# Expert loops that turn and copy tokens four tiles ahead, and results added to x by accumulating transfers

## The chip, the cores and the metric

The kernel runs on one core of a Trainium2 chip. What counts is the time of one execution on the device, in microseconds (us). The kernel before takes 1687.06 us, the median of three runs (1686.94 to 1687.19).

## What is computed

The reference carries a tensor x of 64 × 64 tokens with 128 features (f32) through eight stages, four attentions in turn with four feed-forward stages. Each stage adds its result to x, and normalizes x for its own input. The change touches three of the feed-forward stages. All three have eight experts with weights 128 × 512 and 512 × 128, and a router that picks for every token the one expert (f0) or the two experts (f1, f3) with the highest score:

```python
x = x + _L0_ffn_ref(_layernorm(x), ...)   # f0: top-1 of 8, gelu, no biases
x = x + _L1_ffn_ref(_layernorm(x), ...)   # f1: top-2 of 8, gelu, biases b1, b2
x = x + _L3_ffn_ref(_layernorm(x), ...)   # f3: top-2 of 8, relu, biases; its sum is the output
# one expert:  y = act(x @ W1[e] + b1[e]) @ W2[e] + b2[e];  out += gate * y
```

The fourth, f2, lets 16 experts choose their tokens. It has code of its own, and the change leaves it alone.

## The kernel before

x stays in SBUF as 32 tiles of 128 tokens. A routing step sorts the tokens by expert into tiles of 128 slots (padded: 39 tiles in f0, 71 in f1 and in f3), and writes the normalized tokens with their gates to DRAM (`d_xn`). `m.src` holds for each slot the row to fetch, `m.dst` the row of `d_y` for its result, `m.expert` the expert of each tile.

`experts(k, m)` (from L929) is a software pipeline over the tiles n. Each engine has a program of its own, and semaphores hold them together:

- GpSimd (POOL in the profile) gathers the tokens of tile n+6 (L964) and then scatters the results of tile n to `d_y` (L968). `xs` and `y` are rings of four tiles each. Its program is written out tile by tile.
- TensorE (PE) does for tile n in this order: the up projection of tile n+2 (L998) out of `xsT`, turning the tokens of tile n+3 (L991), and the down projection of tile n (L1006). Its results alternate between two PSUM banks of each kind: `BT` for turned tokens, `BH` for the hidden layer, `BY` for the output.
- ScalarE (ACT) copies the turned tokens of tile n+3 from PSUM into `xsT` (L1037), which has two buffers, computes the activation of tile n+2 (L1047) and copies the weights of the expert of tile n+4 (L1032).
- VectorE (DVE) keeps the gates of tile n+3 (L1086, L1088), reads the expert's number (L1072) and adds the bias to the hidden layer of tile n+2 (L1077), and for tile n adds the second bias (L1104) and multiplies by the gate (L1108). f0 has no biases, so neither L1077 nor L1104.

PE, ACT and DVE run a loop in hardware (`Fori`, in `groups`) whose body is a group of four tiles; the first and the last group stand written out.

Each result has its place in `d_y`: partition, choice, tile. After `experts` comes `combine(k, m, out)` (L1117) in a block of its own, before which all engines meet. SP loads the results in quarters of eight tiles, 512 KB each, four of them for each choice (L1142). GpSimd adds the second choice to x, and DVE the first (L1133; in f0, with one choice, the two share the quarters). Behind it DVE takes the statistics of each tile (`tile_stats`, L85) for the next normalization. In f3 there are none of these; SP stores x as the output (L1146).

Of the kernel before, what the change touches and what calls it, by code (L numbers as in the profile page):

```python
# [15 lines left out]
P = 128  # L16
# [651 lines left out]
def wait(eng, sem, value):  # L668

    if not isinstance(value, int) or value > 0:  # L670
        eng.wait_ge(sem, value)
# [256 lines left out]

def experts(k, m):  # L929

# [6 lines left out]
    with ExitStack() as st:  # L937
        def sb(name, shape, dt=F32):
            return st.enter_context(nc.sbuf_tensor(f"{tag}_{name}", shape, dt))
        xs = sb("xs", [P, RX, GROW])  # L940
        slot_gate = sb("slot_gate", [P, RX])
        xsT = sb("xsT", [P, 2, P])
        w1e = sb("w1e", [P, RT, FF])
# [7 lines left out]
            "x_turned", "x_copied", "w_copied", "up_done", "biased", "activated", "down_done", "y_ready", "gate_kept", "y_summed")]  # L951
        up_read = activated if m.b1 is None else biased

        def groups(eng, body):

            body(0)
            with eng.Fori(1, I - 1) as i:
                body(i)
            body(I - 1, turn=LAST, end=True)
        with nc.Block() as block:  # L960
            @block.gpsimd
            def _(pool):
                def gather(n, u):
                    nc.gpsimd.indirect_dma_start(xs[:, u % RX, :], None, k.d_xn,  # L964
                                                 bass.IndirectOffsetOnAxis(m.src[:, n:n + 1], 0)).then_inc(gathered[u % RX], 16)

                def scatter(n, u):
                    nc.gpsimd.indirect_dma_start(k.d_y, bass.IndirectOffsetOnAxis(m.dst[:, n:n + 1], 0),  # L968
                                                 y[:, u % RT, :], None).then_inc(scattered[u % RT], 16)
                for n in range(AHEAD):  # L970
                    wait(pool, x_turned, n - RX + 1)
                    wait(pool, gate_kept, n - RX + 1)
                    gather(n, n)
                for n in range(N):
                    if n + AHEAD < N:
                        wait(pool, gate_kept, n + AHEAD - RX + 1)
                        gather(n + AHEAD, n + AHEAD)
                    pool.wait_ge(y_ready, n + 1)
                    scatter(n, n)
                for u in range(RT):  # L980
                    pool.wait_ge(scattered[u], 16 * len(range(u, N, RT)))

            @block.tensor
            def _(pe):
# [8 lines left out]
                def up_proj(n, u):  # L993
                    pe.wait_ge(w_copied, n + 1)
                    pe.wait_ge(x_copied, n + 1)
                    wait(pe, up_read, n - 1)
                    for s in range(HS):
                        last = nc.tensor.matmul(BH[u % 2][:, s * P:(s + 1) * P], w1e[:, u % RT, s * P:(s + 1) * P],  # L998
                                                xsT[:, u % 2, :], start=True, stop=True)
                    last.then_inc(up, 1)  # L1000
# [8 lines left out]

                def body(i, turn=RX, end=False):  # L1010
                    for u in range(turn):
                        n = RX * i + u
                        e = expert_of(n)
                        if not end or u + 2 < turn:
                            up_proj(n + 2, u + 2)
                        if not end or u + 3 < turn:
                            turn_x(n + 3, u + 3, i + (u + 3) // RX)
                        down_proj(n, u, e)
# [3 lines left out]
                turn_x(2, 2, 0)  # L1022
                up_proj(1, 1)
                groups(pe, body)

            @block.scalar
            def _(act):
# [6 lines left out]
                def copy_x(n, u):  # L1034
                    act.wait_ge(x_turned, n + 1)
                    wait(act, up, n - 1)
                    nc.scalar.copy(xsT[:, u % 2, :], BT[u % 2][:, 0:P]).then_inc(x_copied, 1)  # L1037

# [9 lines left out]

                def body(i, turn=RX, end=False):
                    for u in range(turn):  # L1050
                        n = RX * i + u
                        if not end or u + 3 < turn:
                            copy_x(n + 3, u + 3)
                        if not end or u + 2 < turn:
                            activate(n + 2, u + 2)
                        if not end:
                            copy_w(n + 4, u + 4)
# [7 lines left out]
                activate(1, 1)  # L1065
                copy_w(3, 3)
                groups(act, body)

            @block.vector
            def _(dve):  # L1070
# [19 lines left out]

                def body(i, turn=RX, end=False):
                    es = [expert_of(RX * i), expert_of(RX * i + 1)] if m.b1 is not None else []
                    for u in range(turn):
                        n = RX * i + u
                        if not end or u + 3 < turn:
                            keep_gate(n + 3, u + 3)
                        if m.b1 is not None and (not end or u + 2 < turn):
                            es.append(expert_of(n + 2))
                            bias(n + 2, u + 2, es[u + 2])
                        dve.wait_ge(down, n + 1)  # L1100
                        wait(dve, scattered[u % RT], 16 * (RX // RT) * i + 16 * (u // RT))
# [13 lines left out]


def combine(k, m, out=None):  # L1117

    nc, tag = k.nc, m.tag
    PARTS, TP = 4, NT // 4  # L1120
    with ExitStack() as st:
        y = st.enter_context(nc.sbuf_tensor(f"{tag}_yback", [P, 2, PARTS, TP, D], F32))
        back = [[k.sem(f"{tag}_y_back{c}{q}") for q in range(PARTS)] for c in range(m.choices)]
        second, summed, stored = [k.sem(f"{tag}_{s}") for s in ("second_added", "x_summed", "out_stored")]
        rows = k.d_y[0:2 * T, :].rearrange("(p c j) d -> p c j d", c=2, j=NT)

        def tiles(q):
            return slice(q * TP, (q + 1) * TP)

        def add(eng, c, q):  # L1130
            eng.wait_ge(back[c][q], 16)
            xs = flat(k.x[:, tiles(q), :])
            return eng.tensor_tensor(xs, flat(y[:, c, q]), xs, ALU.add)  # L1133

        def by_pool(q):
            return m.choices == 2 or q % 2 == 1
        with nc.Block() as block:  # L1137
            @block.sync
            def _(sp):
                for q in range(PARTS):  # L1140
                    for c in reversed(range(m.choices)):
                        sp.dma_start(y[:, c, q], rows[:, c, tiles(q), :]).then_inc(back[c][q], 16)  # L1142
                if out is not None:
                    for q in range(PARTS):
                        sp.wait_ge(summed, q + 1)
                        sp.dma_start(out[:, tiles(q), :], k.x[:, tiles(q), :]).then_inc(stored, 16)  # L1146
                    sp.wait_ge(stored, 16 * PARTS)

            @block.gpsimd
            def _(pool):  # L1150
                for q in range(PARTS):
                    if by_pool(q):
                        add(nc.gpsimd, m.choices - 1, q).then_inc(second, 1)

            @block.vector
            def _(dve):
                def measure(q):
                    if m.choices == 1 and by_pool(q):
                        dve.wait_ge(second, sum(by_pool(c) for c in range(q + 1)))
                    else:  # L1160
                        dve.wait_ge(summed, sum(m.choices == 2 or not by_pool(c) for c in range(q + 1)))
                    for t in range(TP):
                        tile_stats(k, q * TP + t)
                for q in range(PARTS):
                    if m.choices == 2:
                        dve.wait_ge(second, q + 1)
                    if m.choices == 2 or not by_pool(q):
                        add(nc.vector, 0, q).then_inc(summed, 1)
                    if out is None and q:
                        measure(q - 1)  # L1170
                if out is None:
                    measure(PARTS - 1)

# [43 lines left out]
def moe_top1(k, weights):  # L1217

    nc = k.nc
    with ExitStack() as st:  # L1220
# [7 lines left out]
        experts(k, m)  # L1228
        combine(k, m)

# [401 lines left out]
def moe_langs(k, weights):  # L1632
# [3 lines left out]
    with ExitStack() as st:  # L1636
# [36 lines left out]
        experts(k, m)  # L1673
        combine(k, m)

# [11 lines left out]
def moe_mlp_router(k, weights):  # L1687

    nc = k.nc
    with ExitStack() as st:  # L1690
# [80 lines left out]
        route(k, st, m, expert_weights(k, w1, w2, "L3_ffn_W1", "L3_ffn_W2") + expert_biases(k, b1_rows, b2, "L3_ffn_b1", "L3_ffn_b2"))  # L1771
        experts(k, m)
        combine(k, m, k.dram["out"].rearrange("b s d -> (b s) d").rearrange("(j p) d -> p j d", p=P))


# [1016 lines left out]
```

## Time and profile before

The profiled execution took 1685.48 us; the profile spans 1683.8 us of it. The mean granted clock of TensorE was 0.865.

| engine | busy us | share of the span | instructions |
|---|---|---|---|
| PE (matmul) | 1139.0 | 68% | 8627 |
| PEld (weight load) | 891.0 | 53% | 8628 |
| DVE | 873.4 | 52% | 2354 |
| ACT | 584.2 | 35% | 1123 |
| POOL | 835.5 | 50% | 942 |

These are means over eight stages. The stretches that belong to the code of the change are these (the loop counts from the first scatter to the end of the last; what follows ends where the next stage begins, or with the program):

| stage | loop | adding the results |
|---|---|---|
| f0 | 121.8 to 238.9 | 238.9 to 262.1 |
| f1 | 487.2 to 712.3 | 712.3 to 741.6 |
| f3 | 1428.7 to 1655.3 | 1655.3 to 1683.8 |

In a timeline each line is one instruction or several merged: its start, its length, the engine, the line of the kernel, what it writes and reads, how many (x1), and in brackets the time its engine idled before it with what ended that. In a line of waits stand the total, the number of times and the longest. The DMA share is the mean busy share of the core's 16 DMA engines.

### The profile page before, as it was taken

The page shows a single profiled execution, that of the slowest core. Times are in us where ns is not written, and L with a number is a line of the kernel's source. Part 1 is how long each engine was busy: PE and PEld are TensorE (multiplying, and loading weights), DVE is VectorE, ACT ScalarE, POOL GpSimd, SP SyncE. Part 2 cuts the span into 40 slices and gives each one's busy share as a digit, 9 for nine tenths or more (in the row PEclk, how much of TensorE's full clock was granted, in tenths as well). Part 3 has the DMA queues.
Part 4 walks back from the last instruction along what each step waited for, and adds up shares of the span by engine and source line. Part 5 has one row for each costly group of instructions (what it writes and reads, how often), then busy time and mean ns, then how long its engine had stood idle before and what let it go on. Part 6 is the DMA issues. An engine that isn't in the chain of part 4 may idle for free. (4 is left out here: it accounts for less than half of the span.)

```text
span 1683.8 us, 30812 instructions
## 1 busy us (share of the span) xinstructions
PE 1139.0 (68%) x8627; PEld 891.0 (53%) x8628; DVE 873.4 (52%) x2354; ACT 584.2 (35%) x1123; POOL 835.5 (50%) x942
## 2 busy tenths in 40 slices
PE   3547744892776666626777889938999784666661
PEld 2437742682566665515444555525788534666661
DVE  4551117467834444468884543335899526344443
ACT  2124425341344444314321222214454531344441
POOL 6235637464245665553535668836444102565654
PEclk9668886996779999958988899978899895899996
DMA  3051116000411111120304445530000013111114
GB/s 106 2 167 40 41 64 119 4 0 4 166 30 38 40 42 39 36 100 11 94 12 112 77 88 104 117 72 5 1 0 0 8 58 119 37 42 39 43 39 161
DMA packets 87353, 95.84 MB, mean 57 GB/s; under 512 B 19509, under 2 KB 66742, under 8 KB 86774
## 3 DMA queue, kind: packets, MB, share of 16 engines
q1 hardware_dynamic: 63542, 53.61, 10.9%
q0 software_dynamic: 22848, 32.85, 9.0%
q10 hardware_dynamic: 896, 8.55, 1.2%
q8 instruction: 34, 0.56, 0.1%
q14 instruction: 33, 0.27, 0.1%
HBM read 65.71 MB, written 29.26 MB: 56 GB/s over the span
## 5 line engine op out<-in xcount | busy, mean ns | idle before, releaser
L998 PE MATMUL psum<-f_xsT,f_w1e 128*128 128x128 f32 x1448 | 222.3, 301 | 174.7 <-ACT f_xsT L1037 115.0
L998 PEld LDWEIGHTS psum<-f_xsT,f_w1e 128*128 128x128 f32 x1448 | 194.6, 209 | 198.8 <-ACT f_w1e L1032 109.5
L968 POOL DMA_INDIRECT d_y<-f_y,f_dst x181 | 178.3, 985 | 198.8 <-DVE f_y L1108 167.2
L964 POOL DMA_INDIRECT f_xs<-d_xn,f_src x181 | 175.4, 969 | 140.6 <-SPq L960 86.3
L1006 PE MATMUL psum<-f_w,f_hT 128*128 x1448 | 200.8, 284 | 3.5 <-ACT f_hT L1047 3.5
L1006 PEld LDWEIGHTS psum<-f_w,f_hT 128*128 128x128 f32 x1448 | 186.1, 201 | 3.8 <-issue 3.8
L490 PE MATMUL psum<-ident,xn 128*128 128x128 f32 x256 | 49.7, 377 | 167.6 <-DVE xn L463 167.5
L1047 ACT ACTIVATE f_hT<-f_hpre 128x512 f32<-128x512 f32 x142 | 89.4, 630 | 210.5 <-DVE f_hpre L1077 180.2
L1077 DVE TENSOR_TENSOR f_hpre<-psum,f_b 128x512 f32<-128x512 f32 x142 | 98.2, 692 | 98.5 <-issue 90.5
L1032 ACT COPY f_w1e<-f_w 128x512 f32 x184 | 113.6, 618 | 66.4 <-PEq L781 48.7
L490 PEld LDWEIGHTS psum<-ident,xn 128*128 128x128 f32 x256 | 43.0, 197 | 173.3 <-ACT xn L504 167.9
L2402 POOL DMA_INDIRECT d_acc<-f_y,f_token x64 | 100.9, 1576 | 48.0 <-DVE f_y L2718 30.4
L1088 DVE SCALAR_TENSOR_TENSOR f_slot_gate<-f_xs,f_second 128x1 f32<-128x1 f32 x142 | 33.6, 237 | 120.2 <-issue 51.6
L2592 ACT ACTIVATE f_g<-psum 128x512 f32<-128x512 f32 x64 | 38.2, 597 | 158.4 <-PE psum L2510 107.5
L1037 ACT COPY f_xsT<-psum 128x128 f32<-128x128 f32 x181 | 47.3, 261 | 104.0 <-PE psum L991 49.2
L2701 DVE TENSOR_TENSOR f_h<-psum,f_g 128x512 f32<-128x512 f32 x64 | 44.0, 688 | 71.0 <-ACT f_g L2592 59.3
L2388 POOL DMA_INDIRECT f_xs<-d_xs,f_token x64 | 62.6, 978 | 27.5 <-issue 18.6
L2510 PE MATMUL psum<-f_xsT,f_wg 128*128 128x512 f32 x128 | 72.4, 649 | 4.3 <-DVE f_h L2701 2.7
L2510 PE MATMUL psum<-f_xsT,f_wu 128*128 128x512 f32 x128 | 70.4, 633 | 0.0
L991 PE MATMUL psum<-ident,f_xs 128*128 128x128 f32 x181 | 53.1, 294 | 23.1 <-DMA f_xs<-d_xn,f_src 23.1
L481 POOL TENSOR_SCALAR xn<-x,ln_mv,ln_rstd 128x128 f32<-128x128 f32 x56 | 47.5, 859 | 42.2 <-DVE ln_rstd L454 42.2
L1104 DVE TENSOR_TENSOR f_y_sum<-psum,f_b 128x128 f32<-128x128 f32 x142 | 40.3, 283 | 53.2 <-PE psum L1006 51.5
(467 smaller groups left out, 2426.2 us busy)
## 6 DMA issues: line engine op xcount, KB each, us to landing
f_yback<-d_y SPq DMA_DIRECT2D x20, 512.0 KB, 6.7
d_xn<-xn ACTq DMA_DIRECT2D x3, 2080.0 KB, 11.7
f_w<-in_L_ffn_W SPq DMA_DIRECT2D x2, 2048.0 KB, 8.6
a_v<-in_ctx SPq DMA_DIRECT2D x4, 1024.0 KB, 7.9
f_wg<-in_WgT SPq DMA_DIRECT2D x16, 256.0 KB
f_wu<-in_WuT SPq DMA_DIRECT2D x16, 256.0 KB
f_wd<-in_WdT SPq DMA_DIRECT2D x16, 256.0 KB
f_xs<-d_xn,f_src POOLq DMA_INDIRECT x181
```

The source lines that it names most:

```text
L490: last = nc.tensor.transpose(k.bank[g][:, i * P:(i + 1) * P], k.xn[:, g * TPC + i, :], k.ident[:])
L964: nc.gpsimd.indirect_dma_start(xs[:, u % RX, :], None, k.d_xn, bass.IndirectOffsetOnAxis(m.src[:, n:n + 1], 0)).then_inc(gathered[u % RX], 16)
L968: nc.gpsimd.indirect_dma_start(k.d_y, bass.IndirectOffsetOnAxis(m.dst[:, n:n + 1], 0), y[:, u % RT, :], None).then_inc(scattered[u % RT], 16)
L991: nc.tensor.transpose(BT[u % 2][:, 0:P], xs[:, u % RX, 0:D], k.ident[:]).then_inc(x_turned, 1)
L998: last = nc.tensor.matmul(BH[u % 2][:, s * P:(s + 1) * P], w1e[:, u % RT, s * P:(s + 1) * P], xsT[:, u % 2, :], start=True, stop=True)
L1006: last = nc.tensor.matmul(BY[u % 2][:, 0:D], hT[:, u % RT, s, :], m.w2[:, bass.ds(e * FF + s * D, D)], start=s == 0, stop=s == HS - 1)
L1032: nc.scalar.copy(w1e[:, u % RT, :], m.w1[:, bass.ds(e * FF, FF)]).then_inc(w_copied, 1)
L1047: nc.scalar.activation(hT[:, u % RT].rearrange("p s t -> p (s t)"), src, m.act).then_inc(activated, 1)
L1077: nc.vector.tensor_tensor(hpre[:, u % 2], BH[u % 2][:].rearrange("p (s t) -> p s t", s=HS), bc(m.b1[:, bass.ds(e * HS, HS)], (P, HS, P), 2 ...
L2388: nc.gpsimd.indirect_dma_start(xs[:, e % 2, t, :], None, k.d_xs, bass.IndirectOffsetOnAxis(token[:, e, t:t + 1], 0)).then_inc(gathered[e % ...
L2402: nc.gpsimd.indirect_dma_start(k.d_acc, bass.IndirectOffsetOnAxis(token[:, e, t:t + 1], 0), y[:, e % 2, t, :], None, compute_op=ALU.add).t ...
L2510: last = nc.tensor.matmul(k.bank[bank][:], w[:, u, s * P:(s + 1) * P], xsT[:, u, :], start=True, stop=True)
```

## The change

The `xsT` ring grows from two to four buffers. PE and ACT turn and copy the tokens of tile n+4, not n+3, in the body of tile n; the prologue turns and copies one more tile. The last two groups stand outside the loop, and a test on the tile number says which steps exist. On DVE the bias of tile n+2 comes ahead of the gate of tile n+3. GpSimd's lead of six tiles and the rings of `xs` and `y` stay.

`combine` is gone, with its buffer and its block. At the end of its program in `experts`, GpSimd waits for the scatters and then issues transfers that add rows of `d_y` to x in SBUF (`accum_op=ALU.add`), the second choice first, then the first choice quarter by quarter, each behind the second choice's quarter. DVE takes the statistics of a quarter once the first choice's transfer has landed; in f3 SP then stores it. In the call of `experts` f3 passes the output.

```diff
-        xsT = sb("xsT", [P, 2, P])
+        xsT = sb("xsT", [P, RT, P])
...
             body(0)
-            with eng.Fori(1, I - 1) as i:
+            with eng.Fori(1, I - 2) as i:
                 body(i)
-            body(I - 1, turn=LAST, end=True)
+            body(I - 2)
+            body(I - 1, turn=LAST)
+
+        def exists(n):
+
+            return not isinstance(n, int) or n < N
+
         with nc.Block() as block:
+            @block.sync
+            def _(sp):
+                if out is not None:
+                    for q in range(PARTS):
+                        sp.wait_ge(back[0][q], 16)
+                        sp.dma_start(out[:, tiles(q), :], k.x[:, tiles(q), :]).then_inc(stored, 16)
+                    sp.wait_ge(stored, 16 * PARTS)
...
                 for u in range(RT):
                     pool.wait_ge(scattered[u], 16 * len(range(u, N, RT)))
+                rows = k.d_y[0:2 * T, :].rearrange("(p c j) d -> p c j d", c=2, j=NT)
+                for c in reversed(range(m.choices)):
+                    for q in range(PARTS):
+                        if c + 1 < m.choices:
+                            pool.wait_ge(back[c + 1][q], 16)
+                        nc.gpsimd.dma_start(k.x[:, tiles(q), :], rows[:, c, tiles(q), :], accum_op=ALU.add).then_inc(back[c][q], 16)
+                for q in range(PARTS):
+                    pool.wait_ge(back[0][q], 16)
...
-                        if not end or u + 2 < turn:
+                        if exists(n + 2):
                             up_proj(n + 2, u + 2)
-                        if not end or u + 3 < turn:
-                            turn_x(n + 3, u + 3, i + (u + 3) // RX)
+                        if exists(n + 4):
+                            turn_x(n + 4, u + 4, i + 1)
                         down_proj(n, u, e)
...
                 def copy_x(n, u):
                     act.wait_ge(x_turned, n + 1)
-                    wait(act, up, n - 1)
-                    nc.scalar.copy(xsT[:, u % 2, :], BT[u % 2][:, 0:P]).then_inc(x_copied, 1)
+                    wait(act, up, n - RT + 1)
+                    nc.scalar.copy(xsT[:, u % RT, :], BT[u % 2][:, 0:P]).then_inc(x_copied, 1)
...
-                        if not end or u + 3 < turn:
-                            copy_x(n + 3, u + 3)
-                        if not end or u + 2 < turn:
+                        if exists(n + 4):
+                            copy_x(n + 4, u + 4)
+                        if exists(n + 2):
                             activate(n + 2, u + 2)
-                        if not end:
+                        if exists(n + 4):
                             copy_w(n + 4, u + 4)
...
-                        if not end or u + 3 < turn:
-                            keep_gate(n + 3, u + 3)
-                        if m.b1 is not None and (not end or u + 2 < turn):
+                        if m.b1 is not None and exists(n + 2):
                             es.append(expert_of(n + 2))
                             bias(n + 2, u + 2, es[u + 2])
+                        if exists(n + 3):
+                            keep_gate(n + 3, u + 3)
...
-def combine(k, m, out=None):
...
+                if out is None:
                     for q in range(PARTS):
+                        dve.wait_ge(back[0][q], 16)
+                        for t in range(TP):
+                            tile_stats(k, q * TP + t)
```

## Rows read from the trace of the kernel before

**Rows 1.** Busy time by stretch: bounds, length, each engine's busy time, clock, DMA share, GB/s.

```profile
238.90:262.10 23.20, 0.00 (x0) 0.00 (x0) 9.73 (x34) 0.01 (x1) 5.50 (x3) 0.56 0.26 94
...
487.20:712.30 225.10, 150.92 (x1167) 140.02 (x1165) 98.71 (x275) 97.12 (x203) 131.93 (x135) 0.97 0.14 40
712.30:741.60 29.30, 0.00 (x0) 0.00 (x0) 13.69 (x36) 0.00 (x0) 11.23 (x4) 0.51 0.39 146
...
1655.30:1683.80 28.50, 0.00 (x0) 0.00 (x0) 9.13 (x4) 0.00 (x0) 11.30 (x4) 0.50 0.68 224
```

**Rows 2.** The scatter's line in the loops of f0, f1 and f3, ns min/median/max.

```profile
L968 POOL DMA_INDIRECT d_y<-f_y,f_dst x39: 967/986/1007, 121.9 to 237.8; - x39
...
L968 POOL DMA_INDIRECT d_y<-f_y,f_dst x71: 967/987/998, 487.2 to 711.3; - x71
...
L968 POOL DMA_INDIRECT d_y<-f_y,f_dst x71: 963/987/998, 1428.8 to 1654.3; - x71
```

**Rows 3.** POOL in order of time, one group of four tiles in f3.

```profile
1530.23 0.99 POOL L968 DMA_INDIRECT d_y<-f_y,f_dst  x1 [1.86 <-DVE f_y L1108]
1531.52 0.97 POOL L964 DMA_INDIRECT f_xs<-d_xn,f_src  x1 [0.31 <-issue]
...
1536.43 0.98 POOL L968 DMA_INDIRECT d_y<-f_y,f_dst  x1 [1.37 <-DVE f_y L1108]
...
1540.29 0.97 POOL L964 DMA_INDIRECT f_xs<-d_xn,f_src  x1 [0.30 <-issue]
1543.16 0.98 POOL L968 DMA_INDIRECT d_y<-f_y,f_dst  x1 [1.90 <-DVE f_y L1108]
```

**Rows 4.** Who waited for whom in f1's loop.

```profile
POOL d_y L968 <- DVE f_y L1108: 66.6, 37, 5.5
...
PE psum L998 <- ACT f_xsT L1037: 43.5, 30, 3.0
```

**Rows 5.** DVE in order of time, in the same group of f3.

```profile
1533.98 0.22 DVE L1088 SCALAR_TENSOR_TENSOR f_slot_gate<-f_xs,f_second 128x1 f32<-128x1 f32 x1 [1.70 <-issue]
1534.94 0.69 DVE L1077 TENSOR_TENSOR f_hpre<-psum,f_b 128x512 f32<-128x512 f32 x1 [0.74 <-issue]
...
1542.27 0.29 DVE L1104 TENSOR_TENSOR f_y_sum<-psum,f_b 128x128 f32<-128x128 f32 x1 [1.95 <-PE psum L1006]
```

**Rows 6.** PE, ACT and POOL in f0's loop, each in order of time.

```profile
131.12 0.27 PE L991 MATMUL psum<-ident,f_xs 128*128 128x128 f32 x1
131.23 1.06 PE L1006 MATMUL psum<-f_w,f_hT 128*128 x8
...
136.72 0.27 ACT L1037 COPY f_xsT<-psum 128x128 f32<-128x128 f32 x1 [5.51 <-DMA a_circ<-d_w]
...
134.66 0.97 POOL L964 DMA_INDIRECT f_xs<-d_xn,f_src  x1 [0.30 <-issue]
```

**Rows 7.** f0's second gather and its turn; a turn in f3's group.

```profile
112.76 0.95 POOL L964 DMA_INDIRECT f_xs<-d_xn,f_src  x1 [0.30 <-issue]
...
115.33 0.48 PE L991 MATMUL psum<-ident,f_xs 128*128 128x128 f32 x1 [0.80 <-DMA f_xs<-d_xn,f_src]
...
1534.42 0.27 PE L991 MATMUL psum<-ident,f_xs 128*128 128x128 f32 x1
```

**Rows 8.** Behind the last scatter of f1, and SP's stores in f3, in order of time.

```profile
717.12 5.99 SPq L1142 DMA_DIRECT2D f_yback<-d_y  x8
...
737.31 3.18 DVE L85 BATCH_NORM_STATS2 stats<-x 128x6 f32<-128x128 f32 x16
...
1668.54 10.51 SPq L1146 DMA_DIRECT2D out<-x  x4
```

**Rows 9.** DMA queues in 1115:1124 (expert-choice stage) and 717:731; 9 and 14 us.

```profile
q0 software_dynamic: 576, 0.26, 33.8%
q1 hardware_dynamic: 358, 0.18, 7.8%
...
q1 hardware_dynamic: 1152, 4.19, 80.4%
```

More of the change, by code:

```diff
@@ L926, in count_any, with experts @@
     return 13
-def experts(k, m):
+def experts(k, m, out=None):
     nc, tag = k.nc, m.tag
@@ L952, in experts, with tiles @@
         up_read = activated if m.b1 is None else biased
+        PARTS, TP = 4, NT // 4
+        back = [[k.sem(f"{tag}_y_back{c}{q}") for q in range(PARTS)] for c in range(m.choices)]
+        stored = k.sem(f"{tag}_out_stored")
+        def tiles(q):
+            return slice(q * TP, (q + 1) * TP)
         def groups(eng, body):
             body(0)
-            with eng.Fori(1, I - 1) as i:
+            with eng.Fori(1, I - 2) as i:
                 body(i)
-            body(I - 1, turn=LAST, end=True)
+            body(I - 2)
+            body(I - 1, turn=LAST)
+        def exists(n):
+            return not isinstance(n, int) or n < N
         with nc.Block() as block:
+            @block.sync
[5 more added lines that the diff above has]
+                    sp.wait_ge(stored, 16 * PARTS)
             @block.gpsimd
@@ L998, in up_proj @@
                         last = nc.tensor.matmul(BH[u % 2][:, s * P:(s + 1) * P], w1e[:, u % RT, s * P:(s + 1) * P],
-                                                xsT[:, u % 2, :], start=True, stop=True)
+                                                xsT[:, u % RT, :], start=True, stop=True)
                     last.then_inc(up, 1)
@@ L1008, in down_proj, with body @@
                     last.then_inc(down, 1)
-                def body(i, turn=RX, end=False):
+                def body(i, turn=RX):
                     for u in range(turn):
@@ L1023, in _ @@
                 up_proj(1, 1)
+                turn_x(3, 3, 0)
                 groups(pe, body)
@@ L1047, in activate, with body @@
                     nc.scalar.activation(hT[:, u % RT].rearrange("p s t -> p (s t)"), src, m.act).then_inc(activated, 1)
-                def body(i, turn=RX, end=False):
+                def body(i, turn=RX):
                     for u in range(turn):
                         n = RX * i + u
-                        if not end or u + 3 < turn:
-                            copy_x(n + 3, u + 3)
-                        if not end or u + 2 < turn:
+                        if exists(n + 4):
+                            copy_x(n + 4, u + 4)
+                        if exists(n + 2):
                             activate(n + 2, u + 2)
-                        if not end:
+                        if exists(n + 4):
                             copy_w(n + 4, u + 4)
@@ L1066, in _ @@
                 copy_w(3, 3)
+                copy_x(3, 3)
                 groups(act, body)
@@ L1089, in keep_gate, with body @@
                                                        in1=row[:, D:D + 1], op0=ALU.mult, op1=ALU.add).then_inc(gate_kept, 1)
-                def body(i, turn=RX, end=False):
+                def body(i, turn=RX):
                     es = [expert_of(RX * i), expert_of(RX * i + 1)] if m.b1 is not None else []
@@ L1114, in _ @@
                 groups(dve, body)
-def combine(k, m, out=None):
[L1119 to L1143, printed above, removed]
-                    for q in range(PARTS):
[L1145 to L1172, printed above, removed]
@@ L1228, in moe_top1 @@
         experts(k, m)
-        combine(k, m)
 def make_attention_tables(k):
@@ L1673, in moe_langs @@
         experts(k, m)
-        combine(k, m)
 def expert_weights(k, w1, w2, n1, n2):
@@ L1771, in moe_mlp_router @@
         route(k, st, m, expert_weights(k, w1, w2, "L3_ffn_W1", "L3_ffn_W2") + expert_biases(k, b1_rows, b2, "L3_ffn_b1", "L3_ffn_b2"))
-        experts(k, m)
-        combine(k, m, k.dram["out"].rearrange("b s d -> (b s) d").rearrange("(j p) d -> p j d", p=P))
+        experts(k, m, k.dram["out"].rearrange("b s d -> (b s) d").rearrange("(j p) d -> p j d", p=P))
 def masked_attention(k, w):
```

## The prediction

> **What bounds the kernel now.** I read the busy times by stretch first [rows 1], because the chain of waits follows only the last per cent of the span. Only three stages hold code that the change touches: the three expert loops f0, f1 and f3, with the adding of results behind each. In f1's loop, 225.1 us long, PE is busy for 150.92, POOL for 131.93, DVE for 98.71 and ACT for 97.12; f3 runs the same code on as many tiles. No engine is full, so latency sets the pace. The scatters' first and last starts give that pace: f0 (237.8 − 121.9) / 38 = 3.05 us a tile, f1 (711.3 − 487.2) / 70 = 3.20, f3 (1654.3 − 1428.8) / 70 = 3.22 [rows 2].
>
> Next I read POOL's order of time over one group of four tiles in f3 [rows 3]. Scatter to scatter is 1543.16 − 1530.23 = 12.93 us. In it stand four pairs of gather (0.97) and scatter (0.99), each with 0.30 of issue behind it: 2.57 a tile, 10.28 a group. That is POOL's floor. The rest is two pauses, 1.86 and 1.37 long where 0.30 would be normal, both ended by DVE's y. Over f1's loop POOL waited 37 times, 66.6 us, for y [rows 4]: about one pause to two tiles. Two causes stand behind them.
>
> The first is the **order of work on DVE and the two xsT buffers**. At the turn of its loop DVE idles 1.70 before the small gate operation, and then 0.74 more for the expert number before the bias [rows 5]. In f1's loop PE waited 30 times, 43.5 us, for ACT's copy of x before an up projection [rows 4]. That copy stands directly ahead of its use, in the same body, because only two buffers exist.
>
> The second I hold for the deeper one: **PE's completions reach others late while POOL issues indirect DMAs back to back**. In f0 PE turned a tile at 131.12 to 131.39. ACT, which had nothing else to do, started its copy at 136.72 after idling 5.51. POOL's unbroken chain of DMAs ended at 134.66 + 0.97 = 135.63, 1.09 earlier [rows 6]. In the f3 group DVE's idle of 1.95 before the y sum ended at 1542.27 [rows 5], 1.01 behind POOL's last DMA, which started at 1540.29 and ended at 1541.26 [rows 3]. So a chain of m tiles is followed by a pause in which the completions arrive and y is made: per tile 2.57 + e/m. With m = 2 and f1's 3.20, e = 2 × 0.63 = 1.26. With that e, f0's 3.05 gives m = 2.6.
>
> **The change, part by part.**
>
> *Loops.* Four xsT buffers let ACT copy tile n+4 while PE works at n+2; the work per tile is the same instructions in another order. PE's wait for x goes. What is late next? A chain lasts as many tiles as have completed down projections when it begins, plus those whose completion still gets through early in it. With two result banks (BY), two tiles can be complete ahead; the third may start as soon as DVE has read the first. PE does it in 1.06 us [rows 6] if it is not held by its up projection, which now it isn't. The fourth needs the second to be read, one DVE round of about 2.05 later (my estimate: gate, bias, y sum and y, 0.22, 0.69, 0.29 [rows 5] and as much again for y, with some 0.6 for the expert number, of 0.74), and is then too late to be heard. So I take m = 3, bounds 2 and no pause at all: 2.57 + 1.26 / 3 = 2.99, say 3.00 a tile.
> - f1: 224.1 − 70 × 3.00 = 14.1 less. f3: 225.5 − 210.0 = 15.5 less. f0: 115.9 − 38 × 3.00 = 1.9 less; it has neither bias nor y sum and its chains are nearly that long now. Sum −31.5.
>
> Edits at no cost: bias ahead of gate on DVE (the sum of the two stays; POOL's gather waits for a gate three tiles old at least); one more turn and copy in the prologue, 0.27 and 0.26, beside the same gathers; the Fori is shorter by one group that stands written out. Moving turn_x one tile earlier shortens a gather's lead. A gather started at 112.76 had its turn at 115.33, 2.57 later [rows 7]. The gather that starts at 1531.52 [rows 3] would be turned where PE turned another tile at 1534.42 [rows 7], 2.90 later. So 0.3 us of cover is left; if the gather is late, it holds PE's down projection of the same body, the turn being queued ahead of it, and through it DVE's y. I take 0 here, with the loss of all the gain as the other end (rival B).
>
> *Adding the results.* Before, the block ends, the engines meet, and SP issues the first load of results at 717.12, 4.8 us behind the end of the last scatter (711.3 [rows 2] + 0.97); the last statistics end at 737.31 + 3.18 = 740.49 [rows 8], the stretch at 741.6 [rows 1]. That is 29.3 us in f1, 23.2 in f0 (four transfers), 28.5 in f3 with stores. After, POOL waits for its scatters (landing about 1.6 behind the end of the instruction, by the gather: 115.33 − 112.76 − 0.95 [rows 7]) and issues the first accumulating DMA at once; packets some 1.7 later, so 3.3 after the scatter's end. The adds on POOL and DVE vanish; what is left is X us for each 512 KB.
>
> X isn't in the trace, since no accumulating DMA into SBUF runs. From below: loads of 512 KB, 4096 B packets, 1152 of them at 80.4% of 16 engines in 14 us: 16 × 14 × 0.804 / 1152 = 156 ns, eight per engine and transfer: 1.25, with gaps 1.27 us. From above: the expert-choice stage scatters with accumulation, 512 B packets, 576 at 33.8% of 9 us: 84 ns; the plain 512 B packets beside them 31 ns (358 at 7.8%) [rows 9]. A factor 2.7 on 1.27 gives 3.4. If the cost is by 512 B piece, it is 8 × 8 × 0.084 = 5.4. I take 2.6: an accumulating packet reads the result and x where a plain one reads once, so twice 156 ns, and this lies nearest to the ratio row. The ends stay 1.27 and 5.4.
> - f1: 712.3 + 3.3 + 8 × 2.6 = 736.4; statistics of the last quarter 1.6, DVE reading behind the transfers; up to 3 until the engines meet: 741.0 against 741.6, −0.6.
> - f0: 238.8 + 3.3 + 4 × 2.6 = 252.5, + 1.6 + 2.4 = 256.5 against 262.1, −5.6.
> - f3: 1655.3 + 3.3 + 20.8 = 1679.4. The out stores of three quarters share the DMA engines, 3 × 1.27: 1683.2. The last store then takes what it takes today, from the end of SP's last issue, 1668.54 + 10.51 = 1679.05 [rows 8], to 1683.8: 4.8. So 1688.0, +4.2.
> - Sum −2.0. Twenty transfers in all: each 0.1 us on X is 2 us on the time.
>
> The Trainium skill, DMA: Bandwidth & Descriptors, section "Anatomy of one DMA — SWDGE (gpsimd) path", gives a transfer issued by GpSimd about 2.0 us fixed and then bytes at 436 GB/s, 1.20 us for 512 KB; the plain loads of this trace, 1.27, agree with the second part, and no accumulating one is there to compare. Its section "Issuing engine by pattern" calls the hardware queues (SP) generally faster, which speaks against the change. If each transfer paid the fixed part as well, X would be 3.2 and the time by that estimate some 12 us above my forecast.
>
> **The sum.** Against the profiled execution (1685.48, span 1683.8): 1685.48 − 31.5 − 2.0 = 1652.0. It lies 1.6 under the median of the runs, 1687.06; that is inside what I can tell, so I predict 1652.
>
> **The rivals.**
> - *A: the pauses go altogether.* If PE's late completions are only a consequence of its being late itself, POOL's floor sets the pace: 70 × 2.57 = 179.9 and 38 × 2.57 = 97.7. Gains 44.2, 45.6 and 18.2, with −2.0: 1575.5. For it: DVE's round of 2.05 and PE's 2.4 (two projections of 1.06, one turn of 0.27) fit under 2.57. Against: the 5.51 idle of rows 6, in a stage with half of DVE's work and PE long done.
> - *B: the loops don't move.* The completions come with POOL's chains, of two tiles, whatever the order, or the gather's 0.3 us of cover is used up: 1683.5. For it: both pause rows end 1.0 to 1.1 behind POOL. Against: f0, with less work on DVE, has longer chains now.
> - *C, slower: accumulation is paid by 512 B piece.* X = 5.4: 20 × 2.8 = 56 more, 1708. The place is behind the last scatter of each stage, where nothing else runs to hide it. It outweighs the loops from X = 2.6 + 33.5 / 20 = 4.3. For it: POOL's accumulating packets of 84 ns against 31. Against: those write into DRAM at scattered rows, these into SBUF in rows of 4096 B.
> - *D: accumulation at the plain rate.* X = 1.27: 20 × 1.33 = 26.6 less, 1625. For it: if an addition streams in the engine, bytes decide. The Trainium skill's fit named above would give this too. Against: the same ratio of 84 to 31.
>
> **How the numbers follow.** Forecast 0.47 (its own range, X from 1.6 to 3.4 and m from 2.5 to 4: 1630 to 1670), A 0.17, B 0.12, C 0.12, D 0.12. For eight in ten I take 1580 to 1686: it leaves out C and half of A. This kernel's measurement can tell about 0.2%, 3.4 us, from no change. Faster: forecast, A, D and a third of B, 0.80. Same: the rest of B, 0.08. Slower: C, 0.12.
>
> **What would show it.** In the loops: scatters 3.0 us apart; POOL's waits for y about one to three tiles, some 23 instead of 37; PE's wait for f_xsT before the up projection near nothing; DVE's wait for the down projection grown, its ends 1.1 behind POOL's chains. 2.6 a tile would show A, 3.2 B; idle before the turn put down to the gather would show that B's cause is the lead. In the additions: the time between landings of two accumulating transfers is X directly; f1's stretch behind the last scatter should be some 29 us and f3's some 33. I am wrong most easily in X, which counts twenty times, and in m.

## The result, and the profile after

The changed kernel took 1694.74 us, the median of eight runs, against 1687.07 us before (eight runs): a ratio of 1.005, 95% interval 1.0029 to 1.007. The forecast was 1652. Its profiled execution spans 1691.9 us, 8.1 more than before. The scatters of its three loops, the groups that answer to [rows 2]:

```profile
L988 POOL DMA_INDIRECT d_y<-f_y,f_dst x39: 967/987/1009, 121.6 to 233.3; - x39
...
L988 POOL DMA_INDIRECT d_y<-f_y,f_dst x71: 967/987/999, 481.9 to 711.9; - x71
...
L988 POOL DMA_INDIRECT d_y<-f_y,f_dst x71: 964/987/1000, 1429.3 to 1658.6; - x71
```

f0 went from 115.9 to 111.7 us (2.94 a tile), f1 from 224.1 to 230.0 (3.29), f3 from 225.5 to 229.3 (3.28). One loop gained 4.2 us, the two long ones lost 5.9 and 3.8. The stretches behind the last scatters and f1's loop, as in [rows 1]:

```profile
234.30:258.10 23.80, 0.00 (x0) 0.00 (x0) 6.58 (x32) 0.00 (x0) 3.69 (x5) 0.53 0.48 91
481.90:712.90 231.00, 162.14 (x1164) 145.27 (x1162) 92.10 (x275) 97.07 (x200) 131.96 (x135) 0.96 0.13 39
712.90:742.90 30.00, 0.00 (x0) 0.00 (x0) 6.58 (x32) 0.02 (x1) 7.12 (x8) 0.51 0.74 142
...
1659.60:1691.90 32.30, 0.00 (x0) 0.00 (x0) 0.00 (x0) 0.00 (x0) 7.04 (x8) 0.50 0.90 197
```

They are 0.6, 0.7 and 3.8 us longer than before. The changes of loops and stretches add up to +10.6; the stages between came 2.5 us sooner.

The waits in f1's loop, against [rows 4] (in total, times, longest):

```profile
POOL d_y L988 <- DVE f_y L1138: 67.3, 31, 5.6
...
PEld psum L1019 <- DMA f_xs<-d_xn,f_src: 10.0, 22, 1.9
```

POOL waits 31 times for y where it waited 37 times, but one wait is now 2.17 us and not 1.80, and the total stays. With its other idle time before scatters POOL lost 85.1 us in f1 (67.3 and 17.8 put down to issue) against 79.2 before (66.6 and 12.6): 5.9, all that the loop grew by. PE's long wait for ACT's copy of x (43.5 us) isn't among the waits any more. PE now waits for gathers a little, as the shorter lead would have it.

The counts 31 and 37 leave out the pauses that this view puts down to issue. Counted by their length alone, every gap of more than 0.5 us between two of POOL's DMAs in f1's loop, the pauses went from 39 (64.2 us, 1.65 each) to 36 (69.1 us, 1.92 each). In f3 they went from 36 (1.79 each) to 35 (1.94), in f0 from 21 (1.55) to 19 (1.46). So the mean chain in f1 grew from 1.8 tiles to 1.9 only. By the length of the chain ahead of the pause, in f1:

| tiles in the chain | before: chains, mean pause us | after |
|---|---|---|
| 1 | 11, 1.56 | 12, 1.76 |
| 2 | 27, 1.60 | 16, 1.65 |
| 3 | 1, 3.74 | 8, 2.70 |

The chains of three tiles that the forecast wanted do appear, but a longer pause stands behind each, and chains of one tile are as many as before.

What the pause behind such a chain is made of, for one of three tiles in f3 (POOL, then PE, then DVE):

```profile
1527.52 0.98 POOL L988 DMA_INDIRECT d_y<-f_y,f_dst  x1 [1.91 <-DVE f_y L1138]
...
1533.94 0.97 POOL L984 DMA_INDIRECT f_xs<-d_xn,f_src  x1 [0.30 <-issue]
1537.97 0.99 POOL L988 DMA_INDIRECT d_y<-f_y,f_dst  x1 [3.06 <-DVE f_y L1138]
```

```profile
1530.11 1.15 PE L1026 MATMUL psum<-f_xsT,f_w1e 128*128 128x128 f32 x8 [0.83 <-issue]
1531.40 0.33 PE L1019 MATMUL psum<-ident,f_xs 128*128 128x128 f32 x1
```

```profile
1536.35 0.69 DVE L1107 TENSOR_TENSOR f_hpre<-psum,f_b 128x512 f32<-128x512 f32 x1 [5.19 <-remote]
...
1537.08 0.28 DVE L1134 TENSOR_TENSOR f_y_sum<-psum,f_b 128x128 f32<-128x128 f32 x1
1537.40 0.29 DVE L1138 TENSOR_SCALAR f_y<-f_y_sum,f_slot_gate 128x128 f32<-128x128 f32 x1
```

And ACT (`remote` stands where the view finds no work that ended shortly before the wait did):

```profile
1536.34 0.27 ACT L1066 COPY f_xsT<-psum 128x128 f32<-128x128 f32 x1 [4.41 <-remote]
```

POOL's chain ends at 1534.91. ACT and DVE, which wait for two different operations of PE, start within 0.01 us of each other, 1.43 and 1.44 later. It isn't PE's work that sets this moment: the up projection that the bias waits for had ended at 1531.26, the turn that the copy waits for at 1531.73. Then the bias (0.69), the y sum and y follow before POOL can scatter. The pause is 3.06: with 7.39 of chain, 10.45 us for three tiles, 3.48 a tile. The prediction had set 2.99.

The trace also records the moment of each update of a semaphore, and there the lateness shows by itself. Between 1531.26 and 1535.38 PE ended six pieces of work: up projection, turn and down projection of one body, and the same of the next. Five of them ended within POOL's chain, but none of the updates is recorded before its end. All six come between 1536.21 and 1536.63, in PE's order. Over f1's loop all updates of the down projections are recorded. In the changed kernel 45 of 70 come more than 0.5 us behind the end of their matmul, all but one of them while POOL idles, by the median 1.21 us behind the end of its chain. In the kernel before they are 39 of 70, at 1.05 us.

### The profile page after: what moved, and what is told of

The parts are those of the page before. It is cut to its first block and busy times, and to the rows that moved or that the text cites. A ratio compares the mean times of both kernels' runs of the same rounds, so it can differ in the third digit from the quotient of the medians.

```text
span 1691.9 us, 30612 instructions
## 1 busy us (share of the span) xinstructions
PE 1160.6 (69%) x8627; PEld 899.2 (53%) x8628; DVE 842.5 (50%) x2344; ACT 582.5 (34%) x1120; POOL 825.4 (49%) x952
## 5 line engine op out<-in xcount | busy, mean ns | idle before, releaser
L1026 PE MATMUL psum<-f_xsT,f_w1e 128*128 128x128 f32 x1448 | 226.5, 305 | 142.0 <-ACT f_w1e L1061 83.3
L1026 PEld LDWEIGHTS psum<-f_xsT,f_w1e 128*128 128x128 f32 x1448 | 198.0, 212 | 164.8 <-issue 80.4
L1034 PE MATMUL psum<-f_w,f_hT 128*128 x1448 | 212.5, 294 | 3.2 <-ACT f_hT L1076 2.9
L1034 PEld LDWEIGHTS psum<-f_w,f_hT 128*128 128x128 f32 x1448 | 191.4, 206 | 7.5 <-issue 4.1
L1019 PE MATMUL psum<-ident,f_xs 128*128 128x128 f32 x181 | 56.8, 314 | 36.8 <-DMA f_xs<-d_xn,f_src 32.1
L85 DVE BATCH_NORM_STATS2 stats<-x 128x6 f32<-128x128 f32 x224 | 46.8, 279 | 61.2 <-DMA x<-d_y 34.5
```

Of the source, the lines that this page charges most:

```text
L1019: nc.tensor.transpose(BT[u % 2][:, 0:P], xs[:, u % RX, 0:D], k.ident[:]).then_inc(x_turned, 1)
L1034: last = nc.tensor.matmul(BY[u % 2][:, 0:D], hT[:, u % RT, s, :], m.w2[:, bass.ds(e * FF + s * D, D)], start=s == 0, stop=s == HS - 1)
```

## The experiments

The runs fell into two conditions, which the kernel before shows best: it took 1687.07 beside the result, 1688.74 beside e1 to e4, 1679.81 beside e9 and e10 and 1683.95 beside e18, but 1567.31 beside e5 to e8, 1568.61 beside e11 to e13, 1566.05 beside e14, 1568.46 beside e15 and e16, and 1568.6 beside e17. I call the first *late* and the second *prompt*: in the traces of the second the completions of PE come at once where POOL issues its chains (in e7 and e15 each of f1's 70 recorded updates of a down projection comes within 0.02 us of its matmul's end). The granted clock of TensorE doesn't make the difference: f1's loop had 0.97 before and 0.96 after in the late condition and 1.00 in e15, but e5, prompt, had 0.97 there and no late completion. e9 and e11 ran on one and the same chip in different conditions, so it isn't a property of a chip. Ratios below are always against the kernel before in the same condition, on the same chip.

**e1, the changed loops alone** (late). The loops of the change, with `combine` as before.

> The changed expert loops (four xsT buffers, turn and copy at n+4, bias ahead of gate on DVE), with combine as before. Theory L (the loops of f1 and f3 got slower because POOL's longer chains of DMAs hold back PE's completions longer, and f0's got faster): f0's first to last scatter about 112 us, f1's about 230, f3's about 229, against 115.9, 224.1 and 225.5 before; time +3 to +5 us, about 1691. Theory M (the loops lose only beside the accumulating transfers, or the trace of after was one bad execution): f1 and f3 at 224 to 226, f0 112, time 1683.

Measured: 1685.23 against 1688.74, ratio 0.9978 (0.9958 to 0.9998). In the trace f0 took 111.2 us, f1 227.4, f3 230.8: theory L in every loop (−4.7, +3.3, +5.3). The time is below its range all the same. Part of that lies behind the last scatters, whose code is the one of before: 22.7, 28.3 and 27.4 us against 23.2, 29.3 and 28.5, in sum 2.6 less (the loops of e8, turned ahead too, are followed by 22.4, 28.2 and 27.6). The rest isn't settled in this condition, where the runs of the kernel before spread over 1675.79 to 1695.22.

**e2, accumulating transfers alone** (late).

> The loops as before, the results added by accumulating transfers. Theory L: all three loops at 3.05, 3.20, 3.22 us a tile as before; behind the last scatter 23.8, 30.0 and 32.3 us as in the changed kernel against 23.2, 29.3 and 28.5: +5 us, about 1692. Theory M: the whole +8 us comes from here, about 1695.

Measured: 1689.19, ratio 1.0007 (0.9983 to 1.003). Loops 118.0, 225.1 and 226.7 us; behind the last scatter 23.1, 30.1 and 32.4 us. Theory M falls: the transfers alone don't carry the loss. Nor do the two parts add up to the whole: −0.2% (e1) and +0.1% (e2) against the +0.5% of the result and the +0.15% of e9. The statistics of f1 start as the quarters land:

```profile
732.43 1.64 DVE L85 BATCH_NORM_STATS2 stats<-x 128x6 f32<-128x128 f32 x8 [19.23 <-DMA x<-d_y]
734.88 1.65 DVE L85 BATCH_NORM_STATS2 stats<-x 128x6 f32<-128x128 f32 x8 [0.81 <-DMA x<-d_y]
737.33 1.65 DVE L85 BATCH_NORM_STATS2 stats<-x 128x6 f32<-128x128 f32 x8 [0.81 <-DMA x<-d_y]
739.82 1.64 DVE L85 BATCH_NORM_STATS2 stats<-x 128x6 f32<-128x128 f32 x8 [0.84 <-DMA x<-d_y]
744.88 0.22 DVE L437 TENSOR_TENSOR ln_mv<-stats 128x32 f32<-128x32 f32 x1 [3.42 <-PEq L60]
```

X is 2.45 us, against the 2.6 of the sum. The next stage starts 3.42 behind the last statistics.

**e3, y ahead of the bias** (late).

```diff
-  bias(n + 2); keep_gate(n + 3); y_sum(n); y(n)
+  y_sum(n); y(n); bias(n + 2); keep_gate(n + 3)
```

> The changed loops with combine as before, but on DVE the y sum and y of tile n stand ahead of the bias of tile n+2 and the gate of n+3. Theory L (the pauses of POOL grew because y is queued behind a bias whose up projection is heard late): the bias (0.69 us) and its wait leave the pause, 30 pauses times 0.7 to 1.0 us: f1 and f3 at 200 to 210 us, time about 1650. Rival G (the gather, turned 2.9 us after its start, holds PE; PE's idle before the turn is 24.6 us in f1): no gain, f1 stays at 225 to 230.

Measured: 1701.91, ratio 1.0079 (1.005 to 1.0108). f1 took 239.3 us and f3 241.4, slower than in any other late run. Both theories missed. The waits in f1:

```profile
ACT f_hT L1054 <- DVE f_hpre L1085: 135.4, 69, 3.6
DVE f_y_sum L1107 <- PE psum L1012: 93.7, 40, 3.7
...
POOL d_y L974 <- DVE f_y L1111: 77.0, 40, 4.8
```

ACT's wait for the bias doubled (62.3 in the changed kernel). The y sum now waits for a late down projection with the bias queued behind it. So moving the bias out of the pause saves nothing as a whole: in both orders that were tried something is held back behind a late completion.

**e4, the loads of before in the block of experts** (late). SP, POOL and DVE get the programs of `combine` at the end of their programs in `experts`:

```diff
+  for u in range(RT):
+      sp.wait_ge(scattered[u], 16 * len(range(u, N, RT)))
+  ... SP's loads (seven buffers, the eighth quarter waits for the first to be added), adds on POOL and DVE, as in combine
-  combine(k, m)
```

> Loops as before. The plain loads by SP and the adds on POOL and DVE stay, but they stand in the block of experts, so that SP loads as soon as the scatters have landed (the last of eight quarters into the buffer of the first, for room). If the meeting of the engines cost what it took between the last scatter and the first load (4.8 us in f1 and f3, 8.3 in f0, less some 2 for the scatter's landing): 3 + 3 + 6 less, about 1675. Rival: the engines' meeting at the end takes as much longer as is saved ahead, time unchanged at 1687.

Measured: 1674.37, ratio 0.9922 (0.9895 to 0.9948). Behind the last scatter f0 takes 19.7 us, f1 24.8, f3 23.8. The first load of f1:

```profile
709.01 0.97 POOL L1003 DMA_INDIRECT d_y<-f_y,f_dst  x1 [0.30 <-issue]
711.38 6.66 SPq L989 DMA_DIRECT2D f_yback<-d_y  x8
```

It starts 1.40 behind the scatter's end, against 4.8 before. So the gain that the change looks for in leaving out the meeting of the engines is there, 13 us; in the change the doubled price of each transfer eats it.

**e5, POOL idles behind each scatter** (prompt).

```diff
                     scatter(n, n)
+                    pool.wait_ge(scattered[n % RT], 16 * (n // RT + 1))
```

> The kernel before, but POOL waits behind each scatter until it has landed, so that its DMAs come in chains of two (2.3 us) with about 1.5 to 1.9 us of idle between. Theory S (completions of PE reach others late while POOL issues DMAs without a break): no wait for PE of 1.5 us or more is left on ACT and DVE in the loops; the pace is POOL's own, 0.3 + 0.97 + 0.3 + 0.99 + 1.6 = 4.1 us a tile, f1's loop about 290 us, and no wait of POOL for y beyond a few tenths. Rival (PE or DVE themselves are late): waits of 2 to 5 us for PE remain beside it and the pace is above 4.5.

Measured: 1758.62; loops at 3.66, 3.69 and 3.68 us a tile, POOL's own pace. I had put it at 4.1 because I counted 0.3 of issue beside the wait for the landing, though the whole pause is 1.5 long, and because the last six tiles have no gather. It met the condition in which nothing is late, so it says nothing of S.

**e6, the gathers taken off POOL** (prompt).

```diff
+            @block.sync
+            def _(sp):
+                for n in range(N):
+                    wait(sp, x_turned, n - RX + 1)
+                    wait(sp, gate_kept, n - RX + 1)
+                    sp.dma_start(xs[:, n % RX, :], k.d_xn[(n % 32) * P:(n % 32 + 1) * P, :]).then_inc(gathered[n % RX], 16)
```

> The kernel before, but the tokens of each tile come by a plain load that SP issues from 128 consecutive rows: the gather by index is left out, so wrong tokens are worked on, in the same amount. POOL issues only scatters, 1.29 us each. Theory S: with POOL idle about half of the time the long waits go, and the pace is set by DVE and PE, 2.3 to 2.6 us a tile: f1's loop 165 to 185 us, f0's 90 to 100. Rival (the order on DVE, PE and ACT sets 3.2): f1 stays above 210.

Measured: 1540.68; 1.88 us a tile in f0, 2.66 in f1. With POOL half idle, PE sets the pace of f0 (it is busy for 70.0 of 71.4 us). In f1 no engine is full (PE 144.8 of 185.9 us). That DVE's order of work sets 2.66 there is likely from e8 and e15 below, not shown by this run.

**e7, GpSimd's transfers without the addition** (prompt).

> The loops before and the transfers of d_y into x issued by GpSimd, but without the addition (x is overwritten by the results: the sum is left out). If the addition makes the price, the transfers land 1.27 us apart as SP's did; if GpSimd's issuing makes it (0.85 to 0.93 us busy for each), they stay near 2.46 or the second choice's chain of waits sets 1.5 to 2.

Measured: 1548.48. POOL, waiting for each of the second choice's transfers in f1:

```profile
649.47 0.53 POOL L1002 DMA_DIRECT2D x<-d_y  x1 [2.14 <-DMA x<-d_y]
650.72 0.53 POOL L1002 DMA_DIRECT2D x<-d_y  x1 [0.72 <-DMA x<-d_y]
652.00 0.53 POOL L1002 DMA_DIRECT2D x<-d_y  x1 [0.75 <-DMA x<-d_y]
653.26 0.53 POOL L1002 DMA_DIRECT2D x<-d_y  x1 [0.73 <-DMA x<-d_y]
```

They come 1.26 apart, as SP's loads did. The addition alone takes a transfer of 512 KB from 1.26 to 2.45 us, a factor 1.94; who issues it costs nothing here. The condition isn't the reason: in e15, prompt, the accumulating transfers are 2.5 apart as well.

e7 also has the loops of before, in the prompt condition: 90.2, 187.0 and 185.8 us (2.37, 2.67 and 2.65 a tile) against 115.9, 224.1 and 225.5. That is some 102 of the 120 us between the conditions. The chain of gathers and scatters in the expert-choice stage takes 217.9 us from first to last, against 232.3 in the late trace of before: 14 more.

**e8, turning ahead alone** (prompt). As e1, with DVE's order as before.

> The kernel before with four xsT buffers and turn and copy at n+4, but DVE's order as before (gate ahead of bias), combine as before. If turning ahead is what lengthens f1 and f3: both at 227 to 231 us as in the loops-only run, f0 at 111 to 112. If the order on DVE is, then f1 and f3 at 224 or below, f0 still 111 to 112.

Measured: 1565.69 against 1567.31, ratio 0.9991 (0.9978 to 1.0005); f0 2.43 us a tile, f1 2.65, f3 2.72. Its two cases were meant for late completions. What it does show is the loop without them: 0.5 to 0.6 us a tile faster than e1's in all three. Beside e7, whose loops are those of before, it also shows that turning ahead alone gains nothing where nothing is late (2.37, 2.67, 2.65).

**e9, the changed kernel again** (late).

> The changed kernel itself, on whatever chip it meets. On a chip like that of the runs e1 to e4, where completions of PE come late in POOL's chains and the kernel before takes about 1687: +0.5%, loops of f1 and f3 at 3.28 us a tile. On a chip like that of e5 to e8, where no completion is late and the kernel before takes 1567: theory P (what remains there is POOL's 2.57 a tile and DVE's turn of the loop) gives the loops at 2.57 to 2.65, so 0 to 10 us less from the loops, and +4 from adding the results as in e2: 1561 to 1571. Rival (the gather's lead of 2.9 us is too short once the pace is 2.6): loops above 2.75 a tile, time above 1575.

Measured: 1681.46 against 1679.81, ratio 1.0015 (0.9993 to 1.0036); f1 at 3.24, f3 at 3.21. On this chip the loss is not to be told from none. The intervals of the two late results together reach from −0.1% to +0.7%.

**e10, the hybrid** (late).

> f0 with the changed loop, f1 and f3 with the loops before, and the plain loads and adds inside the block of experts (as e4). On a chip like that of e1 to e4: e4's 1674 less f0's 4 us = 1670. On a chip like that of e5 to e8: 1567 less 12 to 14 of e4 = about 1554, f0's loop no shorter than 2.4 a tile.

Measured: 1670.46 against 1679.81, ratio 0.9942 (0.9914 to 0.997), less than e4's own 0.8% in its center, so the exchange of f0's loop isn't seen to add anything.

**e11 and e12, e5 and e6 again.** Both met the prompt condition, and gave 1761.76 and 1542.03, as there. e16 and e17 did so too (1543.27, 1544.58).

> As e6 (the gather by index is left out, SP loads consecutive rows), for a chip on which completions come late. Theory S: POOL issues single scatters with idle between, so the loops run as in e6, 1.88 us a tile in f0 and 2.66 in f1, against 3.05 and 3.20 before. Rival S2: f1 above 2.9.

**e13, the changed loops with e4's loads in the block** (prompt).

> The changed loops in all three stages, with the plain loads and adds inside the block of experts. Where completions come late: e1's -0.2% and e4's -0.8% add up to 1672; the hybrid e10 is at the same time or 4 us below, since it keeps f0's gain alone. Where they don't: 1554.

Measured: 1538.28 against 1568.61, ratio 0.9816 (0.9778 to 0.9854), 16 us more than e4 and e1 had led me to expect. The loops of f1 and f3 run at 2.52 and 2.53 a tile. **e14** repeats it on another chip, prompt again: 1537.24 against 1566.05, ratio 0.9813 (0.9796 to 0.9829). It wasn't seen under late completions.

> The kernel of e13 alone. If this call meets the condition in which completions of PE come late (kernel before about 1680 to 1690): 1672, 0.8 to 1.0% below. If it meets the other (before 1568): 1538 as in e13.

**e15, the changed kernel a third time** (prompt).

> The changed kernel. Under late completions (before 1680 to 1690): within 0 to +0.5%, as in e9 and the first result. With none late (before about 1567): f1 and f3 at 2.53 us a tile as in e13 and e14 against the 2.65 of the order of before (e8), 70 x 0.12 x 2 = 17 less, f0 nothing, adding the results +4: about 1554, -0.8%. Rival (the loops of e13 and e14 are quick for another reason than the changed loops): 1567 to 1571.

Measured: 1554.18 against 1568.46, ratio 0.9918 (0.9893 to 0.9943), at the forecast of that case. The scatters of f1, and POOL's waits there:

```profile
L988 POOL DMA_INDIRECT d_y<-f_y,f_dst x71: 966/987/998, 461.5 to 638.1; - x71
```

```profile
POOL d_y L988 <- DVE f_y L1138: 12.8, 12, 5.5
...
PEld psum L1019 <- DMA f_xs<-d_xn,f_src: 1.2, 2, 1.0
```

2.52 us a tile. POOL waits 12.8 us for y where the same code, late, waits 67.3. The gather's lead is no matter, with 1.2 us in all. 2.52 is below the prediction's floor of 2.57, because the last six tiles of a loop have no gather: over f1's loop the floor is (70 × 1.29 + 64 × 1.27) / 70 = 2.45. The changed kernel is 0.8% faster here, and up to 0.7% slower in the other condition.

**e18, e6's kernel once more** (late).

> As e17: under late completions (kernel before above 1670) theory S gives 1.9 us a tile in f0, 2.65 in f1 and f3, time about 1543; rival S2 above 2.9 in f1, time above 1570. With none late it repeats 1543.

Measured: 1561.66, with the kernel before at 1683.95. The scatters of f0, f1 and f3:

```profile
L975 POOL DMA_INDIRECT d_y<-f_y,f_dst x39: 954/957/1210, 120.7 to 192.1; - x39
...
L975 POOL DMA_INDIRECT d_y<-f_y,f_dst x71: 957/957/1089, 437.3 to 623.2; - x71
...
L975 POOL DMA_INDIRECT d_y<-f_y,f_dst x71: 957/957/1102, 1341.7 to 1527.4; - x71
```

71.4, 185.9 and 185.7 us: 1.88, 2.66 and 2.65 a tile, within 0.1 us what e6 had in the prompt condition. None of the 70 updates of f1's down projections is more than 0.21 us late. Theory S holds in the three loops: with POOL's DMAs apart there is nothing late, in the late condition too. Of the 21 us above e6's time 16 lie in the stages between f1 and f3 (from f1's next stage at 656.3 to 1239.0, against 652.4 to 1218.8), where POOL still issues gathers and scatters in chains. From the first of these to the last it takes 231.6 us, as in the late trace of before (232.3), and 219.1 in e6. So this very execution was in the late condition. It is a single execution, and it takes away the gathers together with the unbroken chains. A run that breaks the chains and keeps the gathers (e5) was never seen late, so it isn't separated whether the breaks or the missing gathers help.

## Why the prediction was wrong

**What bounds the kernel.** Right: POOL's DMAs as the floor (2.57 a tile with a gather, 2.45 over f1's loop), the pauses as the rest, and PE's completions held back until POOL's chain ends. The last of these was argued from two rows; the semaphore records and e18 show it. That it is a condition of the run, worth 120 us to the kernel before (1687 against 1567), no trace of before could show.

**The step that failed is the pair of terms in 2.57 + e/m**: the chain that grows to m = 3, and the constant e. Eight chains of f1 did reach three tiles, but the mean stayed at 1.9. With m = 1.9 even an unchanged e = 1.26 gives back all of the forecast gain (2.57 + 0.66 = 3.23). And e isn't constant: taken as the pause less 0.30, it is 1.35 behind two tiles and 2.40 behind three, so a three-tile chain costs 2.57 + 0.80 = 3.37 a tile and a two-tile chain 3.25. The trace of before held this already, in the four three-tile chains of its f1 and f3 with pauses of 3.7 and 3.6 us.

The mean pause in f1 grew by 0.27 us. The semaphore records say where, for the pauses that have a completion of PE recorded (36 of 39 before, 31 of 36 after). From the end of POOL's chain to the first completion of PE it takes 0.86 us before and 0.91 after (0.88 and 0.97 in f3). From there to the next scatter it took 0.84 and now takes 1.17 (0.92 and 1.29 in f3). In f0, which has neither bias nor y sum, this second part stays at 0.78 and 0.79. So the growth lies in what follows the release, with DVE's bias (0.69) ahead of y as the likely piece; no late run has turning ahead without the new order on DVE, so the two aren't separated. f0's chains hardly lengthened (1.8 to 2.0 tiles): its 2.94, against a forecast of 3.00 from m = 3, came of fewer and shorter pauses, so the number was met by luck. Between e1, e9 and the result f1 and f3 vary from 3.21 to 3.30.

**Gather's lead, bias ahead of gate**, at no cost: right where nothing is late. PE's waits for the gather were 1.2 us in the weight loads of f1 there. Late they were 10.0, beside POOL's waits, and no run separates their part in the 5.9 us. DVE's order is worth something after all in the prompt condition: 2.65 in e8, 2.52 in e15.

**X = 2.6**: 2.45 measured. Twice the plain packet was the right estimate, and the ratio of 2.7 from the scattered 512 B packets the wrong one. f1 (+0.7 for −0.6) and f3 (+3.8 for +4.2) came close, in part because errors cancel: the first accumulating transfer landed 7.6 us behind the last scatter's end in f1, where 3.3 + 2.6 = 5.9 had been set. **f0 missed** by 6 us, +0.6 for −5.6: its last statistics, here in order of time, end at 251.76 and the next stage starts at 258.14.

```profile
250.11 1.65 DVE L85 BATCH_NORM_STATS2 stats<-x 128x6 f32<-128x128 f32 x8 [0.81 <-DMA x<-d_y]
...
258.14 0.22 DVE L437 TENSOR_TENSOR ln_mv<-stats 128x32 f32<-128x32 f32 x1 [6.39 <-PEq L60]
```

The meeting of the engines costs 6.4 us there and 3.4 in f1. I had taken 2.4, 4.0 us too little; most of the rest is a late first landing there too (the first statistics start 7.4 us behind the scatter's end). I had taken it so low though the 8.3 us ahead of f0's first load, against 4.8 in f1, showed that f0's is the dear one. It had been moved, not removed.

**The rivals.** B, that the loops don't move because completions come with POOL's chains, is what happened, at a chance of 0.12. I had set f0's longer chains against it, m = 2.6 by the constant e; counted, f0's chains were 1.8 tiles long. Its 1683.5 then lacked f0's 6 us and the loops' loss. A, the pauses go almost altogether, is what the other condition shows: 2.52 a tile, for 2.57. But most of that is the condition's doing, in which the loops of before take 2.67 and 2.65. The range ended 9 us short, as B's time was its upper end with nothing above it for errors of its own.

## What to carry to other kernels

Before pricing a better order, see whether the waits end with the work they wait for or with another engine's pause: two engines that start within 0.01 us of each other, behind different operations, point to the latter. More lookahead then bought longer chains and longer pauses here. Before a model like e/m is used, sort the pauses of the trace by the length of the chain ahead of them, with one threshold for all. When a meeting of engines is merged away, price it at each place from its own row, and look where it is paid next; and try the plain form (e4) before a transfer that adds, which here costs 1.94 of a plain one.

## What the runs showed of the hardware

The same program, unchanged, runs in one of two conditions some 110 to 120 us apart, on the same chip at different times (1679.81 beside e9, 1568.61 beside e11). In the late one, many completions of PE that fall into an unbroken chain of GpSimd's indirect DMAs (45 of 70 down projections in the changed f1) are held and reach ACT and DVE together behind its end, mostly 0.9 to 1.6 us behind it in the changed f1 and up to 5.3 us late (f0's copy of rows 6, 136.72 − 131.39). In the prompt one they aren't late even where POOL's chains are longer (5 pauses in all of f1's loop in e15). What brings on a condition, and what holds the completions, stays open. Where POOL issues only scatters, with idle between, the three loops run alike in both conditions (e6, e18). The condition could not be chosen, so the idling POOL of e5 and the version of e13 were never seen late.
